# A mixed attention and expert kernel on one core: scores from 32-row matmuls in two halves, and the exponent operands made in another order

## The reference

```
log_f = log_sigmoid(fg);  cs = cumsum(log_f)
log_D = where(causal, cs_i - cs_j, -inf) + ig_j
D     = exp(log_D - rowmax(log_D))
C     = (q k^T / sqrt(32)) * D
h     = (C / (max(|rowsum(C)|, exp(-rowmax)) + eps)) v
x     = x + layernorm(h) * ln_scale
```

## Time and profile before

| | |
|---|---|
| median of 3 runs | 1253.69 us (1251.91 to 1255.4) |
| profiled execution | 1241.27 us, span 1239.5 us |
| busy share TensorE / VectorE / ScalarE / GpSimd | 92% / 74% / 68% / 28% |
| mean granted TensorE clock | 0.964 of 2.4 GHz |
| instructions | 21821 |

### The profile page before, as it was taken

The page is one execution under the profiler, slowest core; times in us unless marked ns, Lnnn a source line. Parts: engine busy times, 40 slices in busy tenths (PEclk is TensorE's granted clock), DMA queues, the critical chain, the costliest instruction groups (busy, mean ns, idle before and its releaser), DMA issues. The chain is left out here.

```text
span 1239.5 us, 21821 instructions
## 1 busy us (share of the span) xinstructions
PE 1137.4 (92%) x7861; PEld 996.7 (80%) x7861; DVE 919.4 (74%) x2215; ACT 837.6 (68%) x1441; POOL 341.8 (28%) x319
## 2 busy tenths in 40 slices
PE   2748999999989999989989897999999999999996
PEld 1436776886777777777868787999999999999996
DVE  5885696686777777866955564888888888888883
ACT  3526556566476556565664353999999999999994
POOL 7121221510510412313113020233333233333333
PEclk9776999999999999999999898999999999999998
DMA  6110011111010100110001035788888888888872
GB/s 197 34 35 17 34 36 35 36 35 35 35 52 23 65 27 32 46 35 35 19 17 44 1 121 170 219 220 233 239 212 232 244 208 232 244 209 230 246 186 27
DMA packets 141692, 136.17 MB, mean 110 GB/s; under 512 B 48599, under 2 KB 127585, under 8 KB 141585
## 3 DMA queue, kind: packets, MB, share of 16 engines
q1 hardware_dynamic: 122948, 111.68, 28.6%
q0 software_dynamic: 14304, 18.75, 9.2%
q10 hardware_dynamic: 4332, 4.34, 1.0%
HBM read 109.42 MB, written 25.33 MB: 109 GB/s over the span
## 5 line engine op out<-in xcount | busy, mean ns | idle before, releaser
L1358 DVE TENSOR_TENSOR wlo<-big,whi 128x512 fp32r<-128x512 f32 x312 | 219.9, 716 | 21.8 <-ACT whi L1311 14.4
L1311 ACT CAST whi<-big 128x512 fp32r<-128x512 f32 x312 | 191.2, 615 | 6.5 <-PEq L420 5.1
L590 ACT ACTIVATE shared_hraw<-bank,b1s 128x512 f32<-128x512 f32 x128 | 88.1, 688 | 153.9 <-PE bank L1119 153.6
L1283 PE MATMUL bank<-xhi,whi 128*128 128x256 f32 x624 | 175.6, 281 | 6.3 <-DVE xlo L1372 5.1
L1261 PE MATMUL bank<-whi,hhi 128*128 128x256 f32 x624 | 178.1, 285 | 0.0
L1283 PE MATMUL bank<-xhi,wlo 128*128 128x256 f32 x624 | 174.5, 280 | 0.0
L1261 PE MATMUL bank<-wlo,hhi 128*128 128x256 f32 x624 | 174.4, 280 | 0.0
L1261 PE MATMUL bank<-whi,hlo 128*128 128x256 f32 x624 | 174.4, 280 | 0.0
L1283 PE MATMUL bank<-xlo,whi 128*128 128x256 f32 x624 | 174.3, 279 | 0.0
L1333 ACT ACTIVATE hraw<-bank,b 128x256 f32<-128x256 f32 x312 | 147.9, 474 | 36.2 <-PE bank L1283 35.3
L835 DVE TENSOR_TENSOR shared_hlo<-shared_hraw,shared_hhi 128x512 fp32r<-128x512 f32 x128 | 93.1, 731 | 96.4 <-ACT shared_hhi L593 92.9
(11 more groups left out here) (275 smaller groups left out, 2634.6 us busy)
## 6 DMA issues: line engine op xcount, KB each, us to landing
big<-in_L_ffn_W_r_dram SPq DMA_DIRECT2D x78, 1024.0 KB, 7.4
qcT<-sorted_tokens SPq DMA_DIRECT2D x39, 260.0 KB, 2.9
xb<-in_x_dram SPq DMA_DIRECT2D x8, 512.0 KB, 4.6
cb<-in_ctx_dram SPq DMA_DIRECT2D x8, 512.0 KB, 3.5
xr<-in_x_dram SPq DMA_DIRECT2D x8, 512.0 KB, 3.5
out_dram<-base ACTq DMA_DIRECT2D x8, 512.0 KB, 2.9
sorted_tokens<-chunk SPq DMA_DIRECT2D x9, 260.0 KB, 3.4
out_dram<-yt,token POOLq DMA_INDIRECT x78, 4.0
```

The costliest lines, as they stand in the source:

```text
L590: nc.scalar.activation(hraw[:, k % NHB, :], up_bank[k % 2][:, :], ACT.Gelu, bias=b1s[:, k // M, k % M:k % M + 1]).then_inc(gelu_done, 1)
L1283: last = nc.tensor.matmul(ub[:, 0:T], w[i][:, wsl], x_[i][:, k, :], start=k == 0 and t == 0, stop=k == KD - 1 and t == 2)
L1311: nc.scalar.copy(whi[i][:, psl], raw[i][:, psl]).then_inc(t_whi, 1)
L1358: nc.vector.tensor_tensor(wlo[i][:, psl], raw[i][:, psl], whi[i][:, psl].bitcast(fp32), ALU.subtract).then_inc(t_wlo, 1)
```

## The change

Four things are altered. (1) The scores are computed head by head from the 32 partitions that a head fills, with no masked copies: eight matmuls of 32 rows and 128 columns a tile, in two halves of four. In a half, neighbours in program order use the row groups r and r+1 and the banks 2 and 3, so the even heads come to lie in one bank and the odd ones in the other; VectorE's product reads and writes them by that order. TensorE waits for its own first half before the second. (2) For all tiles but the first, the first half stands in front of the exponents, the second behind them; and the two mask matmuls now stand together, then the two exponent matmuls. (3) `rest[:,1]` (L739) moves in front of the `yield`, so that it is made in step `C` and not in `c`, behind the last unit. (4) `EH` goes from 4 to 5: VectorE makes five heads' rows of `exp_rhs`, ScalarE three. The masks, the copies of q, their semaphores and the set-up of `headmask` go; a tile `space` of the same size keeps the addresses.

```diff
-        headmask = A("headmask", [P, HG])
+        A("space", [P, HG])
...
-                nc.gpsimd.memset(headmask[:, :], 1.0)
...
-        EH = NH // 2
+        EH = NH // 2 + 1
...
-                    for r in range(HG):
-                        last = nc.gpsimd.tensor_scalar(qmask[:, 1, r, :], qcT[:, 1, :], headmask[:, r:r + 1], None,
-                                                       ALU.mult)
-                    last.then_inc(qmask_pool, 1)
...
-                    for r in range(HG):
-                        last = ts(qmask[:, 0, r, :], qcT[:, 0, :], headmask[:, r:r + 1], None, ALU.mult)
-                    last.then_inc(qmask_dve, 1)
...
                     own.done(nc.vector.tensor_copy(tail16, rest[:, 0, :]))
-                    yield
                     own.done(stt(rest[:, 1, :], tail16, take_two[:, :], rest[:, 0, :], ALU.mult, ALU.add))
                     dve.sem_inc(rest_ready, 1)
+                    yield
                     own.done(nc.vector.tensor_copy(low16[0:HR, :], rest[0:HR, 1, :]))
...
-                        dve.wait_ge(score_done, J * b + j + 1)
+                        dve.wait_ge(score_done, 2 * (J * b + j + 1))
...
-                            last = stt(ct[:, g * HG:(g + 1) * HG, :],
-                                       banks(b, j)[2 + g][:, :].rearrange("p (h s) -> p h s", s=P), SCALE,
-                                       decay[:, g * HG:(g + 1) * HG, :], ALU.mult, ALU.mult)
+                            last = stt(ct[:, :, :].rearrange("p (i o) s -> p i o s", o=2)[:, :, g, :],
+                                       banks(b, j)[2 + g][:, :].rearrange("p (i s) -> p i s", s=P), SCALE,
+                                       decay[:, :, :].rearrange("p (i o) s -> p i o s", o=2)[:, :, g, :], ALU.mult, ALU.mult)
...
+                    def exponents(j):
+                        cj = slice(j * P, (j + 1) * P)
+                        for g in range(KD):
+                            mm(banks(b, j)[g][:, :], identb[:, :], causal[:, :].unsqueeze(1).to_broadcast([P, HG, P]),
+                               start=True, stop=False)
+                        for g in range(KD):
+                            last = mm(banks(b, j)[g][:, :], exp_lhs[:, cj],
+                                      exp_rhs[:, j, g * HG:(g + 1) * HG, :].rearrange("p h s -> p (h s)"),
+                                      start=False, stop=True)
+                        last.then_inc(exp_done, 1)
+
+                    def score_half(j, half):
+                        cj = slice(j * P, (j + 1) * P)
+                        for g in range(KD):
+                            for odd in range(2):
+                                r = 2 * half + odd
+                                at = (2 * g + half) * P
+                                last = mm(banks(b, j)[2 + odd][:, at:at + P], qcT[r * DH:(r + 1) * DH, KD + g, cj],
+                                          qcT[r * DH:(r + 1) * DH, g, cj], start=True, stop=True)
+                        last.then_inc(score_done, 1)
...
                         if j == 0:
+                            exponents(j)
                             pe.wait_ge(state_ready, b + 1)
-                            pe.wait_ge(qmask_dve, b + 1)
-                            pe.wait_ge(qmask_pool, b + 1)
-                        for g in range(KD):
-                            last = mm(banks(b, j)[2 + g][:, :], qcT[:, KD + g, cj], qmask[:, g, :, cj], start=True, stop=True)
-                        last.then_inc(score_done, 1)
+                            score_half(j, 0)
+                        else:
+                            score_half(j, 0)
+                            exponents(j)
+                        pe.wait_ge(score_done, 2 * (J * b + j) + 1)
+                        score_half(j, 1)
```

More of the change, by code:

```diff
@@ L144, in xattn_moe_kernel @@
         qn = A("qn", [P, J, D])
-        qmask = big[0][:, :].rearrange("p (g r s) -> p g r s", g=KD, r=HG)
         norm_x, norm_u = ((A(f"bn6_{n}", [P, J, 6]), A(f"mv_{n}", [P, J, 2]), A(f"nw_{n}", [P, 5, J])) for n in "xu")
@@ L282, in _ @@
                                         base=0, pattern=[[1, NE], [-1, NE]], channel_multiplier=0)
-                nc.gpsimd.affine_select(out=headmask[:, :], in_=headmask[:, :], compare_op=ALU.is_ge, fill=0.0,
-                                        base=0, pattern=[[-DH, HG]], channel_multiplier=1)
                 nc.gpsimd.affine_select(out=blockmask[:, :, :], in_=blockmask[:, :, :], compare_op=ALU.is_ge,
@@ L295, in _ @@
                     pool.wait_ge(s_const, 2 + r)
-                nc.gpsimd.affine_select(out=headmask[:, :], in_=headmask[:, :], compare_op=ALU.is_ge, fill=0.0,
-                                        base=DH - 1, pattern=[[DH, HG]], channel_multiplier=-1)
                 nc.gpsimd.affine_select(out=blockmask[:, :, :], in_=blockmask[:, :, :], compare_op=ALU.is_ge,
@@ L332, in xattn_moe_kernel @@
         moments_1, q_ready, tr_done, qcT_ready = (sem(n) for n in ("moments_1", "q_ready", "tr_done", "qcT_ready"))
-        qmask_pool, qmask_dve = sem("qmask_pool"), sem("qmask_dve")
         gates_done, logsig_ready, rows_ready, lhs_ready = (sem(n) for n in ("gates_done", "logsig_ready", "rows_ready", "lhs_ready"))
@@ L1026, in back @@
                     yield
+                    def exponents(j):
[17 more added lines that the diff above has]
+                        last.then_inc(score_done, 1)
                     def scores(j):
-                        cj = slice(j * P, (j + 1) * P)
                         if b > 0 and j > 0:
@@ L1034, in scores @@
                             pe.wait_ge(counts_read, b)
-                        for g in range(KD):
-                            mm(banks(b, j)[g][:, :], identb[:, :], causal[:, :].unsqueeze(1).to_broadcast([P, HG, P]),
-                               start=True, stop=False)
-                            last = mm(banks(b, j)[g][:, :], exp_lhs[:, cj],
-                                      exp_rhs[:, j, g * HG:(g + 1) * HG, :].rearrange("p h s -> p (h s)"),
-                                      start=False, stop=True)
-                        last.then_inc(exp_done, 1)
                         if j == 0:
+                            exponents(j)
                             pe.wait_ge(state_ready, b + 1)
-                            pe.wait_ge(qmask_dve, b + 1)
-                            pe.wait_ge(qmask_pool, b + 1)
-                        for g in range(KD):
-                            last = mm(banks(b, j)[2 + g][:, :], qcT[:, KD + g, cj], qmask[:, g, :, cj], start=True, stop=True)
-                        last.then_inc(score_done, 1)
+                            score_half(j, 0)
[4 more added lines that the diff above has]
+                        score_half(j, 1)
                     pe.wait_ge(lhs_ready, b + 1)
```

## The result

The changed kernel took 1217.3 us (median of 4 runs, 1213.29 to 1218.16) against 1254.55 (median of 4, 1251.91 to 1257.42) for the kernel before, a ratio of 0.970 with an interval of 0.967 to 0.973. That is 37 us less. One thing has to be seen first. The profiled execution of the kernel before took 1241.27 us, and that of the changed kernel 1217.44, so the two traces are only 23.8 us apart, while the medians are 37 apart. The trace on which the prediction rests was not one of a typical run.

A forecast was written before the change was run, and what follows sets the result against it. TensorE, busy for 92% of the span, was taken to bound the kernel. Savings of 9.5 + 5.5 + 1.9 + 1.3 = 18.2 us gave a profiled 1223.0 us and a median of 1235.5, range 1226 to 1255.

The forecast's parts named there:

- 1, boundary: Between batch elements: moved rest and five VectorE rows shorten TensorE's wait for ScalarE's L555 copies, saving 9.5 us.
- 2, scores: Score matmuls in five slots a half, 1.15 us a tile against 1.71 before; 5.5 plus 1.9 us saved.
- 3, masked copies: Dropping GpSimd's and VectorE's masked copies saves 1.3 us at the start and nothing in the steady part.
- I take the differences as they are from one to the other: Savings read from the profiled execution, 1241.27 us, were applied unchanged to the median of 1253.69, 12.4 us above.
- all pairs side by side: Rival: all score instructions overlap in pairs, 0.92 us a tile; 24.0 us saved, 1229.7 us; chance 0.16.
- the cap of 0.46 on the third tile: In the third tile VectorE is busy without a gap, which limits any gain from the scores there to 0.46 us.
- loads one after another: Rival: score weight loads don't overlap across row groups, a tile costs 0.43 us more; 1253.5 us; chance 0.21.
- drain: Rival: each change of row group costs 0.2 us, six more a tile in the scores; 1290 us; chance 0.08.
- another chain takes the boundary: Rival: other waits give back half the boundary's gain and the clock takes the rest; 1246 us; chance 0.13.
- L555's wait: Sign: TensorE's wait for ScalarE's copies at the boundary falls to 2 to 3 us from 11.9.
- A half: Sign: half a tile's score matmuls take about 0.8 us from first start to the next matmul, changes included.
- The wait in the second tile: Sign: TensorE's wait at L1071 in the second tile grows to 0.8 to 1.0 us from 0.67.

The follow-up runs named there:

- e13: The changed kernel, nothing edited, run again in a later batch: 1213.57 us beside 1243.44 for the kernel before, ratio 0.977.
- e16: The kernel before with only the rest moved in front of the last unit's difference and five rows on VectorE: 1232.12 us, ratio 0.991.
- e1: The kernel before, unedited, run and profiled again: 1255.23 us, ratio 1.000.
- e4: The changed kernel with the masked copies still made on GpSimd and VectorE, read by nobody: 1232.45 us, ratio 0.982.
- e2: The kernel before with only the rest moved in front of the last unit's difference and five rows on VectorE: 1242.07 us, ratio 0.991.
- e15: The changed kernel with both engines' masked copies still made, read by nobody, in a later batch: 1216.61 us, ratio 0.979.
- e3: The changed kernel with the rest's move and the fifth VectorE row undone, so new scores without masked copies: 1236.73 us, ratio 0.986.
- e17: The changed kernel with all score matmuls in one row group, profiled: 1260.19 us, a single run beside one of 1252.44 for the kernel before.
- e11: The changed kernel with a half's eight score matmuls reordered so that neighbours share a row group and an output bank: 1214.38 us, ratio 0.978.
- e12: The kernel before with only the rest moved in front of the unit's difference, four rows still on VectorE: 1231.72 us, ratio 0.992.
- e8: The kernel before with GpSimd's eight indirect transfers issued behind the values and masked copies of the element after next: 1251.14 us, ratio 0.995.
- e6: The changed kernel with only GpSimd's masked copies still made, read by nobody: 1228.17 us, ratio 0.977.

## Why the prediction was right and wrong

Without the lateness, each part by the kernels that differ by it alone (the batch of e13 to e16), beside the prediction's terms; with it, by those of e1 to e4 and the first measurement:

| part | predicted | without lateness | with lateness |
|---|---|---|---|
| 1, boundary | 9.5 | 11.3 (before to e16) | 13.0 (before to e2) |
| 2, scores | 7.4 | 15.5 (e16 to e15) | 9.6 (e2 to e4) |
| 3, masked copies | 1.3 | 3.0 (e15 to e13) | 15.2 (e4 to after) |
| all | 18.2 | 29.9 | 37.3 |

Without the lateness the parts add up to the last row by the way they are taken, and with it they do within 0.5 us because the first measurement and e1 to e4 agree that closely on the kernel before. Each part is known to about 2 us. The scores win less with the lateness, 9.6 us against 15.5, since TensorE's waits for VectorE's difference grow from 7.2 us in e2 to 11.3 in e4. The split also goes by the order: with the lateness the boundary is worth 13.0 us on the kernel before and 19.4 on e3 (1236.73 less 1217.3). Why was not tried; the granted clock of e3's runs lies lower than that of the others, at 0.948 to 0.959.

The steady part of the traces says it without the start and across batches. From the first product of the third element to that of the eighth, in us:

| kernel | without lateness | with lateness |
|---|---|---|
| before | 433.9 | 444.7 (e1) |
| boundary changed | 423.4 (e16) | 430.0 (e2) |
| all changed, copies kept | 415.9 (e15) | 426.5 (e4) |
| changed | 415.8 (e13) | 416.0 |

The lateness costs 11 us here in the kernel before and in the changed one with the copies kept, 7 in e2, and nothing once the copies are gone.

**"I take the differences as they are from one to the other."** This step, the one from the profiled execution (1241.27) to the median (1253.69), failed first. The 12.4 us between them weren't noise but a mechanism, as e1's trace shows for its 15.4: the late semaphore in front of VectorE's stretch, 1.4 us at each of five places, 2.7 us once, and what the clock made of the holes. The change gives VectorE the lead that hides it: at the end of the stretch the changed kernel has 1.72 us of it without the lateness (e13) and still 1.12 with it (the trace of the changed kernel, whose GELUs waited 1.6 to 2.3 us for "remote" at five elements). Some 7.4 of the 37.3 us are that (37.3 less 29.9). The prediction saw the gap and didn't ask what a trace of the usual time would look like.

**"No wait of TensorE names either in the steady part, so I cost the removal at nothing there"** (part 3) is the step where most of those microseconds went. It is right for the trace read: e15 gives 3.0 us in all against e13, and none of it in the steady part. It is wrong with the lateness, where the copies cost 15.2 us and 1.3 were forecast. The row that should have warned stands above, at 347.20: a lead of 0.41 us at the end of a gapless stretch of 20 us that the copies head. The prediction looked for waits, not for how near the next one was; a hidden piece of work has the price "nothing, until the cover is used up", and the cover here was 0.41 us.

**"In order that makes five slots for the eight of a half: 10 x 0.115 = 1.15 us"** (part 2) was wrong. It is four slots of 0.112: e17 shows that instructions of one row group never start closer than that, and e11, where neighbours share a group, has pairs all the same, so the second group's first instruction starts before the first group's others. The Trainium skill's ("TensorE: Matmul & The Clock Gate", Packing small matmuls) near-full overlap, which the prediction quoted for a rival, is what the runs show. The load time of 0.107 us that the Trainium skill gives for such weights on the same page (LDWEIGHTS), and that the prediction quoted for another rival, is no floor across row groups: 16 loads one after the other would take 1.7 us a tile, and the 16 instructions with their loads take 0.90.

The rival "all pairs side by side" had this right, with 0.92 us a tile, and the rest of the prediction's tile sum held. The 2.90 us of a third tile hold 0.12 of the instruction in front and 0.23 of the one behind; 2.55 are left, less 0.85 of exponents and 0.90 of scores, so the changes of row count took 0.80, the number forecast. A third tile saves 0.55 us, where 0.26 was predicted and 0.49 follows from the rival. By the same measure, e16 to e15, the first tile saves 0.44 (0.39 predicted), the second 0.56 and the fourth 0.54. The second tile's goes into waits, as forecast, so an element should gain 0.44 + 0.55 + 0.54 = 1.53 us. It gains 1.50 (423.4 less 415.9, over five elements; 0.91 was predicted, 1.57 by the rival); the cap of 0.46 on the third tile didn't bind. Of the 17.0 us between the traces of e16 and e15, 2.3 lie in front of the first product, 3.6 in the first two elements (1.9 predicted, 3.8 by the rival), 7.5 in the next five and 3.6 behind, where stretches at the lower clock moved too. The rival's whole sum was 24.0 us; the 29.9 measured without the lateness are 5.9 more, some 2 us in each of the three parts, about as much as each is known to. The rivals "loads one after another" and "drain" are excluded: with 0.64 us a half there is no room for either.

**Part 1** held in its mechanism. The rest runs in the gap at 1.00 us (1.11 predicted), ScalarE's copy for the left operand (L539, L550 before) follows its cast at once, and the move alone gave 9.6 us (e12). The element is 1.66 us shorter (86.26 to 84.6), the number forecast, but by another sum, so the match is in part luck: the hole of 2.30 closes wholly with five rows, and 0.63 us of it come back, since the wait for GpSimd grows from 0.30 to 0.93 at three or four boundaries. This is the rival "another chain takes the boundary", at less than its price: GpSimd's weighted values take 4.91 us beside the moved rest,

```profile
349.59 4.91 POOL L475 TENSOR_TENSOR chunk<-vaug,eexp 128x264 f32<-128x264 f32 x6 [30.90 <-ACT eexp L536]
```

where they took 4.29. The 1.8 us above 9.5 are within what two stretches at the lower clock explain, which make two elements of before 87.6 and 87.5 us long in place of 86.2, while in e16 none of them is longer than 84.8. This was not tried; the sum had allowed 3 us for it.

**The signs.** L555's wait at 2 to 3 us: it is 0 with five rows, 3.2 with four. A half at about 0.8 us with its changes: 0.64. The wait in the second tile at 0.8 to 1.0: 1.02, but in two pieces, 0.34 for ScalarE and 0.68 for VectorE. 512 score matmuls of 32 rows, and no other engine above 85%: so.

## What to carry to other kernels

Before costing a removal at nothing, find the stretch without a gap that the removed work lies in, and the lead at its end: a lead of a few tenths of a microsecond is a term with two values, not a zero. When the profiled execution is 1% off the median of the runs, treat the difference as an unread mechanism: ask for a trace of the usual time, or widen the range by all of it. Compare versions in one batch on one chip: the same change gave 2.3% in one and 3.0% in another, both with tight intervals. And measure a piece from an instruction well in front of it to one well behind it: what a change of row count costs falls on the neighbour.

## What the runs showed of the hardware

- While GpSimd issued eight indirect transfers (each about 1.3 us from start to start), ScalarE's instructions that wait for TensorE started late: in e1 a copy by 1.0 us and the GELU behind it by 2.4. So it was in two batches and in the trace of the changed kernel, at some elements of e17, and not at all in two other batches and the trace of before, with the transfers at the same place. Issuing them elsewhere removed it (e8). The batches ran on different chips; what makes one or the other stays open.
- Float32 matmuls of 32 rows and 128 columns start every 0.112 us in one row group, weight load included (e17); two row groups run side by side, in pairs 6 to 14 ns apart, and the order of issue within eight instructions doesn't matter (e11).
- In e6 a 128x32 operation of VectorE that starts 0.1 us behind the first of GpSimd's masked copies took 0.62 us in place of 0.18, at six elements, and the 128x512 difference beside them 1.06 in place of 0.69. The same 128x32 operation in the middle of the copies took 0.18 (trace of before).
